# Another order of a head pair's steps, 16 of its 80 tiles turned through DRAM instead of 20, and another meeting of attention and output projection

## The reference

```python
k = jnp.einsum('ihd,bpd->biph', W_K, x)      # x: 1 x 2048 x 512, 16 heads of 128
q = jnp.einsum('ihd,bpd->biph', W_Q, x)
v = jnp.einsum('ihd,bpd->biph', W_V, x)
scores = jnp.einsum('biph,biqh->biqp', k, q)
masked = scores * mask - 1e10 * (1.0 - mask)          # causal
attn = jax.nn.softmax(masked / sqrt(128), axis=-1)
z = jnp.einsum('biqp,biph->biqh', attn, v)
out = jnp.einsum('df,bqf->bqd', W_O, z_flat)
x = _layernorm(x + out)
...                                                   # experts, layer norm
```

## Time and profile before

| | us |
|---|---|
| median of 3 runs | 2487.53 (2485.11 to 2492.2) |
| the profiled execution, its own time | 2479.21 |
| its span | 2477.5 |
| PE busy | 2363.9 (95%) |
| DVE busy | 1908.8 (77%) |
| ACT busy | 1437.8 (58%) |

### The profile page before, as it was taken

One profiled execution on the slowest core, in us unless ns is written; L12 is line 12 of the kernel. 1 busy time (PEld: TensorE's weight loads), 2 busy tenths in 40 slices (PEclk: granted clock), 3 DMA queues, 4 the chain that ended last, 5 costly groups with the idle time before them and its releaser, 6 DMA issues. The chain is left out here.

```text
span 2477.5 us, 40499 instructions
## 1 busy us (share of the span) xinstructions
PE 2363.9 (95%) x13306; PEld 2042.9 (82%) x13306; DVE 1908.8 (77%) x3811; ACT 1437.8 (58%) x3216; POOL 469.2 (19%) x526
## 2 busy tenths in 40 slices
PE   7999999999999999999999999799999999999993
PEld 6878888887887887887887887588889999899893
DVE  5787687688588588679669678678748888888885
ACT  4555565455465466456456455455437777777774
POOL 0011011011011011011001101267622111222211
PEclk9999999999999999999999999899999999999997
DMA  6353344345354354444434426488649999999997
GB/s 249 119 176 125 126 156 150 130 136 162 120 154 123 125 172 123 141 145 132 141 120 152 150 90 217 147 290 318 217 129 307 310 320 303 302 314 316 296 313 213
DMA packets 229025, 478.80 MB, mean 193 GB/s; under 512 B 28809, under 2 KB 78345, under 8 KB 218832
## 3 DMA queue, kind: packets, MB, share of 16 engines
q1 hardware_dynamic: 179920, 311.82, 36.5%
q0 software_dynamic: 40256, 101.46, 17.2%
q10 hardware_dynamic: 8640, 62.92, 6.5%
HBM read 336.30 MB, written 148.42 MB: 196 GB/s over the span
## 5 line engine op out<-in xcount | busy, mean ns | idle before, releaser
L573 ACT ACTIVATE probs<-bank,neg_max 128x512 f32<-128x512 f32 (+3 forms) x640 | 395.7, 626 | 105.7 <-DVE neg_max L701 87.7
L695 DVE TENSOR_REDUCE max_part<-bank 128x1 f32<-128x512 f32 (+2 forms) x576 | 352.0, 622 | 33.1 <-PE bank L858 24.8
L586 ACT ACTIVATE pT_hi<-turned 128x512 fp32r<-128x512 f32 (+1 forms) x480 | 238.5, 514 | 190.8 <-PE turned L874 189.3
L845 PE MATMUL bank<-x_sb,w_hi 128*128 128x512 f32 x992 | 310.1, 394 | 12.6 <-DVE x_sb L661 11.7
L707 DVE TENSOR_TENSOR pT_lo<-turned,pT_hi 128x512 fp32r<-128x512 f32 (+1 forms) x480 | 268.2, 574 | 25.9 <-ACT pT_hi L586 23.9
L889 PE MATMUL z_ps<-pT_hi,v_hi 128*128 128x512 f32 (+3 forms) x640 | 254.9, 398 | 32.2 <-DVE pT_lo L707 30.4
L858 PE MATMUL bank<-k_hi,q_hi 128*128 128x512 f32 (+2 forms) x640 | 255.5, 399 | 11.5 <-ACT probs L573 6.7
L2012 DVE TENSOR_TENSOR up_lo<-w_raw,up_hi 128x704 fp32r<-128x704 f32 x256 | 217.3, 887 | 35.6 <-ACT up_hi L1499 35.0
L874 PE MATMUL turned<-ident,probs 128*128 128x128 f32 x1536 | 236.9, 273 | 1.4 <-ACT probs L573 1.3
L889 PE MATMUL z_ps<-pT_hi,v_lo 128*128 128x512 f32 (+3 forms) x640 | 234.1, 366 | 0.0
L858 PE MATMUL bank<-k_hi,q_lo 128*128 128x512 f32 (+2 forms) x640 | 233.9, 366 | 0.0
(11 more groups left out here) (217 smaller groups left out, 5552.6 us busy)
## 6 DMA issues: line engine op xcount, KB each, us to landing
w_raw<-in_w SPq DMA_DIRECT2D x256, 352.0 KB, 5.6
x_sb<-x_parts ACTq DMA_DIRECT2D x60, 1024.0 KB, 6.9
far_dram<-stage SPq DMA_DIRECT2D x160, 256.0 KB, 3.4
probs<-far_dram POOLq DMA_DIRECT2D x160, 256.0 KB, 4.0
w_raw<-in_w SPq DMA_DIRECT2D x128, 256.0 KB, 5.2
rows_in<-gathered_x SPq DMA_DIRECT2D x64, 263.5 KB, 5.4
spread_sb<-inv_dram POOLq DMA_DIRECT2D x64, 256.0 KB, 4.3
z_dram<-z_sb SPq DMA_DIRECT2D x64, 256.0 KB, 2.3
```

The costliest lines, as they stand in the source:

```text
L573: nc.scalar.activation(probs[:, u % 2, r, kc * CHUNK:kc * CHUNK + used], bank[:, job_at["s", h, c, r, kc] % BANKS, 0:used], ACT.Exp, bias= ...
L586: nc.scalar.activation(turned_parts(0, h, c, j), turned_tile(h, c, j), ACT.Copy).then_inc(turn_hi, 1)
L695: nc.vector.reduce_max(max_part[:, row % ROWS, kc:kc + 1], bank[:, job % BANKS, 0:used], axis=AX_X).then_inc(part_done, 1)
L845: mark = nc.tensor.matmul(dst, w_sb[a][:, dt, first:first + DH], x_of(b, dt), start=(dt == 0 and (a, b) == PASSES[0]), stop=(dt == DT - 1 ...
```

## The change

ORDER is another string, with four letters b fewer, so all five engines issue a pair's steps in another sequence. FAR loses key blocks 9 and 10 of chunk 3: 16 far tiles a pair. In the last pair the four far tiles of the last unit (1, 3) are near as well: `is_far` is false for them, PE turns them, and their far block, store and fetch are left out. Two buffers change places in SBUF. Behind the barrier PE waits for POOL's constants only at its first transpose.

```diff
-    "tiittflfffllfffpftelffptlpffffepeeeeeoftleftlfepptefteeplffpeietllofftfpeelfffpffffttpllffteptpiellt"
...
+    "itltfflfffiffffpetetfpllfeefpffeetepotlltffleefppfettleptffpolleetilffeeeffptfplfffftfplftplpeteeitl"
...
-FAR = {2: range(4, 8), 3: range(5, 11)}
+FAR = {2: range(4, 8), 3: range(5, 9)}
...
+    last_unit = max(unit_at, key=lambda unit: unit_at[unit])
+    at_last = {tile for tile in far_at if tile[:2] == last_unit}
...
+        v_sb = [sb(f"v_{n}", [P, TILES, 2 * DH], F32R) for n in ("hi", "lo")]
         q_sb = [sb(f"q_{n}", [P, 2, CHUNK], F32R) for n in ("hi", "lo")]
-        v_sb = [sb(f"v_{n}", [P, TILES, 2 * DH], F32R) for n in ("hi", "lo")]
...
-        def turned_tile(h, c, j):
-            if (h, c, j) in far_at:
+        def is_far(i, tile):
+            return tile in far_at and not (i == PAIRS - 1 and tile in at_last)
+
+        def turned_tile(i, h, c, j):
+            if is_far(i, (h, c, j)):
                 return far_place(h, c, j)
...
-            return [step for step in plan if not (last and step[1])]
+            return [step for step in plan if not (last and (step[1] or step[0] == "blocks" and step[2:] in at_last))]
...
-                    if step[0] == "blocks":
+                    if step[0] == "blocks" and is_far(i, step[2:]):
                         fetch(i, *step[2:])
...
-                if (h, c, j) in far_at:
+                if is_far(i, (h, c, j)):
                     return
...
             def turn_x1(i, k):
+                if i == 0 and k == 0:
+                    pe.wait_ge(pool_const, 5)
                 pe.wait_ge(x1_ready, done(i, k))
...
-            pe.wait_ge(pool_const, 5)
             for k in range(TILES):
```

More of the change, by code:

```diff
@@ L154 @@
 ORDER = (
-    "tiittflfffllfffpftelffptlpffffepeeeeeoftleftlfepptefteeplffpeietllofftfpeelfffpffffttpllffteptpiellt"
-    "flpfetpeelpottefflfptelpeeltfffptllpffeeetfptfllpfeeeftlpfpeeotefftlflipeetpfefbbbbefefbeffltpbbiltl"
-    "ffffwfpptltlptfptelbpletlpetffleffptppeeeoettlffffllptpeeltflpefetlffwppptteleeltfflefpfpetepbbtlltf"
-    "fffelbpbeeptpottllfelbpbtptelplefftpptltlflwwpteppelffettelfptllfptppleeittpblftpllebebftpitplotbflf"
-    "fppltfetleffppetbtbllffpeepfftfeelltlfppptlttepltplltpltlptpplpo"
+    "itltfflfffiffffpetetfpllfeefpffeetepotlltffleefppfettleptffpolleetilffeeeffptfplfffftfplftplpeteeitl"
+    "fffptpleeltpotfflfpleteelptfeffpefteellpftfpbetpellfffteppelteeotlffpltflpefbppieetffbbeefebbtllffbb"
+    "tlffffptffptlflweptptipeelltflfffpetppeeteltoflfpleftfpwpteeeelltffffpptetleellfpbffeftpltblpetpeltb"
+    "ffeefptlfppeeteolbtlfflpetpltlfptppttllfplpwweeeettpfftlllffptppeltteeillpebfpptttlblbflfppbttollfpp"
+    "tfftlpieeffptleltlfpeppttfffleflftptptllleptpltptllptlpeeppo"
 )
-FAR = {2: range(4, 8), 3: range(5, 11)}
+FAR = {2: range(4, 8), 3: range(5, 9)}
 def attention_plan():
@@ L215, in attention @@
     n_far, n_near = len(far_at), len(near_at)
+    last_unit = max(unit_at, key=lambda unit: unit_at[unit])
+    at_last = {tile for tile in far_at if tile[:2] == last_unit}
+    assert min(far_at[tile] for tile in at_last) == n_far - len(at_last)
+    near_in = [near_at, {tile: n for n, tile in enumerate(tile for tile in turn_at if tile not in far_at or tile in at_last)}]
+    assert all(near_in[1][tile] == n for tile, n in near_at.items() if tile[:2] != last_unit)
     FAR_SLOTS = 4
@@ L248, in attention @@
         probs_rest = sb("probs_rest", [P, (50176 + 32768 + 65536 - 141312) // 4], F32)
+        v_sb = [sb(f"v_{n}", [P, TILES, 2 * DH], F32R) for n in ("hi", "lo")]
         q_sb = [sb(f"q_{n}", [P, 2, CHUNK], F32R) for n in ("hi", "lo")]
-        v_sb = [sb(f"v_{n}", [P, TILES, 2 * DH], F32R) for n in ("hi", "lo")]
+        z_sb = sb("z_sb", [P, CHUNK], F32)
         pT_sb = [sb(f"pT_{n}", [P, TURNS, CHUNK], F32R) for n in ("hi", "lo")]
         spread_sb = sb("spread_sb", [P, CHUNK], F32)
-        z_sb = sb("z_sb", [P, CHUNK], F32)
         stage = sb("stage", [P, 2, CHUNK], F32)
@@ L579, in turn @@
                 n = turn_at[h, c, j]
-                if (h, c, j) in far_at:
+                if is_far(i, (h, c, j)):
                     act.wait_ge(far_in[far_at[h, c, j] % FAR_SLOTS], far_count(i, far_at[h, c, j], FAR_SLOTS))
                 else:
-                    act.wait_ge(turn_ready, upto(i, n_near, near_at[h, c, j]))
+                    act.wait_ge(turn_ready, upto(i, n_near, near_in[i == PAIRS - 1][h, c, j]))
                 act.wait_ge(pv_done, upto(i, n_turns, n - ring_back(n)))
-                nc.scalar.activation(turned_parts(0, h, c, j), turned_tile(h, c, j), ACT.Copy).then_inc(turn_hi, 1)
+                nc.scalar.activation(turned_parts(0, h, c, j), turned_tile(i, h, c, j), ACT.Copy).then_inc(turn_hi, 1)
             def first_z_hi(i, n):
@@ L706, in low @@
                 dve.wait_ge(turn_hi, upto(i, n_turns, n))
-                nc.vector.tensor_tensor(turned_parts(1, h, c, j), turned_tile(h, c, j),
+                nc.vector.tensor_tensor(turned_parts(1, h, c, j), turned_tile(i, h, c, j),
                                         turned_parts(0, h, c, j).bitcast(F32), ALU.subtract).then_inc(turn_lo, 1)
```

## The result

The changed kernel takes 2457.36 us (median of 4 runs, 2455.36 to 2464.26), the one before 2489.86 in the same comparison: ratio 0.9871 (0.9844 to 0.9898), 32 us faster. The forecast was a gain of 11 us, 2476.3 us, with a range from 2460 to 2494. Two further comparisons of the same kernel gave 0.9907 (0.9888 to 0.9926) and 0.9878 (0.985 to 0.9906), and the kernel before against itself 0.9993 (0.9973 to 1.0012). So the gain is 22 to 32 us.

A forecast was written before the change was run, and what follows sets the result against it. PE, busy 95% of the span, was taken as the bound, standing mainly for DVE's low parts. 13.2 - 16.0 - 7.0 - 1.4 = -11.2 us from the median 2487.5 gave 2476.3 us, range 2460 to 2494.

The forecast's parts named there:

- Transposes: On PE, 30 more tiles turned outside the last unit at 0.44 us each: 13.2 us added.
- So PE's standing falls by 2.7 - 0.7 = 2.0 us a pair, of 4.1 visible: Where chunk 3 begins: DVE relief saves 2.7 us, bank waits cost 0.7; over 8 pairs -16.0 us.
- all 4.1 go: Bound on the pairs' gain: all of PE's visible standing of 4.1 us a pair disappears, -33 us.
- DVE's excess: Where chunk 3 begins, DVE has 8 us more work than PE, at most 5.3 in the new list; drop 2.7 a pair.
- Banks: First scores of new rows in chunk 3 wait longer for a free bank: 0.7 us a pair, half of 1.5.
- The last unit: Last pair's last unit with all tiles near takes 16.7 us, gaining 5.9; with 1.1 ahead of it, -7.0 us together.
- The meeting: At the barrier after attention, PE starts the projection when ACT does, no longer waiting for POOL's constants: -1.4 us.
- Behind the meeting PE is at its limit: After the barrier PE is the bound, so the gain made before it is passed on to the total time.
- all stalls of chunk 3 go: Rival: the stalls where chunk 3 begins vanish entirely, -30 us, 2457 us; chance 0.13.
- The stalls only move: Rival: PE stands as long at other steps; only last unit and meeting gain, +4.8, 2492 us; chance 0.18.
- the banks decide: Rival: first scores of new rows in chunk 3 pay the whole 1.5 us a pair, +20, 2508 us; chance 0.12.
- Trips through DRAM: Rival: far tiles' DRAM trips, some 9 us, arrive late and ACT stands 3.7 us; no time of its own.

The follow-up runs named there:

- e10: Old string with 16 far tiles, old end and wait, but the new string's last 120 steps of a pair; 194.6 us a pair, ratio 1.0007 to the kernel before.
- e9: Old string with 16 far tiles, old end and wait, but the new string's first 255 steps; 195.4 us a pair, ratio 1.0037 to the kernel before.
- e1: Kernel before with only four letters b (key blocks 9 and 10 of chunk 3) left out; 195.9 us a pair, ratio 1.0082 to the kernel before.
- e8: Changed kernel with four far blocks a pair put back, 20 far tiles; 193.8 us a pair, ratio 0.9967 to the kernel before.
- e16: Changed kernel with four more far blocks a pair left out, 12 far tiles; 192.6 us a pair, ratio 0.9929 to the kernel before.
- e4: New string with 16 far tiles, but the far last unit, wait and buffer places of the kernel before; 191.3 us a pair, ratio 0.9922 to it.
- e2: Kernel before, 20 far tiles, plus the near last unit, late wait for POOL's constants and exchanged buffers; 193.0 us a pair, ratio 0.9966 to it.
- e13: Changed kernel with three moves in chunk 3 (two exponentials ahead of turns, a value product ahead of a score); 192.2 us a pair, ratio 0.9897 to the kernel before.
- e12: Changed kernel with only the second weight split moved behind row 2's exponentials and following low parts; 196.4 us a pair, ratio 1.0025 to the kernel before.

## Why the prediction was wrong

The direction held. The sum was too small by one term, PE's standing in the pairs, and the last unit was off the other way, by less; and the comparisons gain 0 to 11 us more behind attention, which I can't place.

*Transposes: right.* 30 tiles at 0.44 us, +13.2; work a pair rose from 184.0 to 185.8.

*"So PE's standing falls by 2.7 - 0.7 = 2.0 us a pair, of 4.1 visible": this step failed.* It fell by 3.7, -29.5 over eight pairs and not -16.0. Two things are wrong in it. First, the 4.1 is only what the view of waits shows; by starts PE stood 9.5 us a pair, so the bound "all 4.1 go" was no bound. Second, I looked at one stretch. Where chunk 3 begins, the net was only -0.9: low parts -2.2 (forecast -2.7), banks and other scores +1.4 (forecast +0.7, at worst +1.5). The other 2.8 us came from the stretches ahead of it (-1.5 and -0.3) and behind it (-1.1), which I had passed over since no single wait there is long: tile (1, 2, 1) alone stood 1.0 us a pair. e10 shows the last of these by itself (-1.3), e9 the first two.

*The reason given for it: half right.* "The forecast is wrong if DVE's excess isn't what makes PE stand." In the old sequence fewer far blocks gave nothing (e1: +0.9 us of standing), in the new one four blocks are worth 3.9 us (e8) and the next four 0.7 (e16). My reading, which no run tests alone: the excess acts only where the sequence has no other wait at that place and enough PE work stands between a near tile's turn and its product. Shown is that neither the new string with 20 tiles (193.8 us a pair) nor the old with 16 (195.9) shortens a pair, and the two together do (191.6).

*Banks: right in place, the size near the worst bound and not half of it.* The three stalls stand where 1.4, 1.4 and 1.6 us of work were counted, at 1.08, 1.10 and 0.62 us a pair.

*The last unit: mis-sized.* In the unit -4.0 and not -5.9: 18.3 us where 16.7 were forecast, at full clock, since the near tiles do wait for low parts there (four times, 0.3 to 0.5 shown). Ahead of it about -0.3 and not -1.1. How the gain divides between the two is firm to 1 or 2 us only: in the later profiles the unit took 20.6 us in the kernel before and 19.4 and 19.6 in the changed one, with PE joining at the same time. With the new string the near tiles are not even its cause (e4: 17.3 us with the far ones); with the old string the new end was worth 6.6 with the wait (e2).

*The meeting: right,* -1.1 for -1.4; PE starts 0.4 us behind ACT.

With the measured terms the sum is 13.2 - 29.5 - 4.3 - 1.1 = -21.7, which is the 21.7 us between the two traces at the first projection matmul, and gives 2465.8 from the median of 2487.5. (The -0.3 is what the other terms leave.) The unprofiled runs show more: the 13 of the changed kernel have a median of 2458, 28 to 32 below the kernel before in the same comparisons (2486.3 to 2489.9). The 0 to 11 us that are missing by the three comparisons lie behind attention, and the profiles can't settle them: there one kernel's executions differ by 17 us. The prediction had two steps there. "Behind the meeting PE is at its limit" isn't so: between 2000 and 2200 us PE was busy 190 of 200 us in one execution. "The exchange of buffers costs nothing that I see" holds for the pair's period (e4) and was not tested behind attention. Median less first projection matmul is 889.7, 897.3 and 889.4 us in the changed kernel, 895 to 900 in the six other kernels that have the exchange and a trace that can be read, and 894 to 905 in those that don't. So the exchange may be worth a few us, and doesn't explain 889 by itself. This stays open.

Of the rivals, "all stalls of chunk 3 go" had the time (2457) and not the mechanism: its stalls did not go, they changed from low parts to banks, and the gain came from elsewhere. "The stalls only move" and "the banks decide" are refuted for this string. Yet in e13 the stalls moved, and in e12 a bank decided (4.2 us of standing a pair at the first score of unit (1, 3)). Trips through DRAM did not become late (3.1 and 3.6 us for 3.4 and 4.0).

## What to carry to other kernels

Measure an engine's standing by starts, over the whole period, before forecasting what a reordering takes away: the list of waits shows the long ones and hides many small ones, here more than half. Choose an order and the number of side steps in it together: either alone shortened no pair here. Before moving a step that two engines share (a high part on one, a low part on the other), look at what stands ahead of its first half and behind its second.

## What was unexpected of the hardware

A stall costs more than it shows: the first matmul behind a wait starts the next one 0.33 us later, where the one after follows in 0.24 (734.47, 734.80, 735.04 in the changed kernel). In pairs 1 to 6 of the kernel before this holds for matmuls of 512 columns behind gaps too short to be listed as well: behind the 7 of 0.01 to 0.05 us the next start came after 0.33, and behind the 379 under 0.01 after 0.23. So even such a wait costs 0.1.

The granted clock fell to half of full behind a long stall. After 3.57 us without a matmul in e12 it was 0.50 for the next 3.7 us, and matmuls of 512 columns started 0.43 us apart. In the last unit of the kernel before, the stalls of 2.37 and 2.51 us had the same spacing behind them (1567.86, 1568.29, 1568.72), and that is part of what the unit had to lose. The stalls of up to 1.75 us in the changed kernel left the clock at 1.00.
